# A graph stage of two convolutions and routing: its first norm measured one stage earlier, four row buffers, a pipeline three steps deep

## What is computed

```python
x = x + _L0_gnn_ref(_layernorm(x), adj, ...)      # attention over adj, and an MLP
x = x + _L0_ffn_ref(_layernorm(x), ...)           # slice attention
x = x + _L1_gnn_ref(_layernorm(x), ..., adj, adj)  # two graph convolutions
x = x + _L1_ffn_ref(_layernorm(x), ...)           # shared expert and top 2 of 8 experts

def conv(x, w_rel, w_root, b):                    # in _L1_gnn_ref
    out = jnp.einsum('bnd,de->bne', x, w_root) + b
    for r in range(R):
        agg = jnp.einsum('bij,bid->bjd', masks[r], x) / deg[r]
        out = out + jnp.einsum('bjd,de->bje', agg, w_rel[r])
    return out
h = jax.nn.elu(conv(encoded_spans, w_rel1, w_root1, b1))
h = jax.nn.elu(conv(h, w_rel2, w_root2, b2))
```

## Time and profile before

| what | us |
|---|---|
| median of three executions | 3094.94 |
| span of the profiled execution | 3076.7 |
| attention and MLP stages | 0 to 785 |
| slice stage | 785 to 1654 |
| graph stage, with the shared part | 1654 to 2339 |
| schedule, experts, combine | 2339 to 3077 |

### The profile page before, as it was taken

The page is one execution under the profiler, slowest core; times in us unless marked ns, Lnnn a source line. Parts: engine busy times, 40 slices in busy tenths (PEclk is TensorE's granted clock), DMA queues, the critical chain, the costliest instruction groups (busy, mean ns, idle before and its releaser), DMA issues. The chain is left out here.

```text
span 3076.7 us, 86393 instructions
## 1 busy us (share of the span) xinstructions
PE 2732.4 (89%) x28365; PEld 2234.3 (73%) x28366; DVE 1965.2 (64%) x6886; ACT 1490.2 (48%) x2994; POOL 1438.8 (47%) x2156
## 2 busy tenths in 40 slices
PE   8999999999799999999996777777567999999798
PEld 4666665799577777777775777667456888888687
DVE  5666665677787888878884677777633444444332
ACT  3444454555465666656563444444333444444343
POOL 5555554333233333333332477677730555555543
PEclk9999999999999999999998777777678999999899
DMA  1111111000000000000000111112301222222254
GB/s 48 34 34 34 34 31 28 1 0 0 1 0 0 0 0 0 0 0 0 0 0 22 31 44 50 42 50 85 88 24 53 75 70 75 74 70 76 70 156 133
DMA packets 158078, 117.85 MB, mean 38 GB/s; under 512 B 20150, under 2 KB 145593, under 8 KB 158010
## 3 DMA queue, kind: packets, MB, share of 16 engines
q1 hardware_dynamic: 140602, 81.02, 9.6%
q0 software_dynamic: 17408, 35.95, 3.4%
HBM read 68.36 MB, written 48.56 MB: 38 GB/s over the span
## 5 line engine op out<-in xcount | busy, mean ns | idle before, releaser
L781 POOL TENSOR_TENSOR s_sw<-s_expo,s_rsum 128x512 f32<-128x512 f32 x128 | 133.5, 1043 | 491.8 <-DVE s_rsum L1026 491.8
L1873 ACT ACTIVATE e_hidden<-e_ps,e_b1g 128x512 f32<-128x512 f32 x288 | 191.6, 686 | 286.4 <-PE e_ps L61 192.6
L1851 POOL DMA_INDIRECT token_y<-e_y,e_rows x288 | 283.1, 983 | 78.0 <-issue 69.0
L1239 POOL DMA_INDIRECT sorted_z<-r_z,r_rows x256 | 258.5, 1010 | 75.4 <-issue 75.4
L1907 PE MATMUL e_ps<-expert_w,e_hidden 128*128 x2304 | 284.9, 276 | 7.8 <-issue 7.6
L1907 PEld LDWEIGHTS e_ps<-expert_w,e_hidden 128*128 128x128 f32 x2304 | 276.2, 192 | 15.6 <-issue 9.3
L427 DVE TENSOR_REDUCE a_V<-a_ps_s 128x8 f32<-128x1024 f32 x128 | 156.9, 1226 | 175.2 <-PE a_ps_s L366 175.2
L291 ACT ACTIVATE a_probT<-a_ps_st 128x1024 f32<-128x1024 f32 x128 | 131.1, 1024 | 202.5 <-PE a_ps_st L374 202.5
L366 PEld LDWEIGHTS a_ps_s<-a_nT 16*128 16x128 f32 x2048 | 135.9, 187 | 91.4 <-issue 55.5
L1948 DVE TENSOR_TENSOR e_biased<-e_ps,expert_b 128x512 f32<-128x512 f32 x72 | 49.8, 692 | 234.8 <-remote 120.2
L366 PE MATMUL a_ps_s<-a_nT 16*128 16x128 f32 x2048 | 185.1, 299 | 11.3
(11 more groups left out here) (399 smaller groups left out, 8114.1 us busy)
## 6 DMA issues: line engine op xcount, KB each, us to landing
e_z<-sorted_z SPq DMA_DIRECT2D x72, 260.0 KB
c_y<-token_y SPq DMA_DIRECT2D x22, 512.0 KB, 4.1
X<-in_x_dram SPq DMA_DIRECT2D x32, 256.0 KB, 2.8
a_adj<-in_adj_dram SPq DMA_DIRECT2D x32, 256.0 KB, 2.8
g_adj<-in_adj_dram SPq DMA_DIRECT2D x32, 256.0 KB
out_dram<-X SPq DMA_DIRECT2D x32, 256.0 KB
c_y_s<-token_y SPq DMA_DIRECT2D x10, 512.0 KB
token_y<-e_y,e_rows POOLq DMA_INDIRECT x288
```

The costliest lines, as they stand in the source:

```text
L781: nc.gpsimd.tensor_tensor(sw[p][:, :, :], expo[p][:, :, :], rsum[p][:, 1, :].unsqueeze(2).to_broadcast([T, HEADS, C]), ALU.mult).then_inc( ...
L1239: nc.gpsimd.indirect_dma_start(sh.sorted_z, bass.IndirectOffsetOnAxis(ap=rows[p][:, e * GB + piece:e * GB + piece + 1], axis=0), zr[p][:, ...
L1851: nc.gpsimd.indirect_dma_start(sh.token_y, bass.IndirectOffsetOnAxis(ap=rows[p][:, b:b + 1], axis=0), y[p][:, b, :], None).then_inc(y_scat ...
L1873: nc.scalar.activation(hidden[p][:, c, :], ps_1[c % 2][:, :], ACT.Gelu, bias=b1g[p][:, c:c + 1]).then_inc(s["hidden_done"], 1)
```

## The change

In the slice stage, `bn_stats` and `bn_aggr` of graph t-7 (whose X is complete) are added to DVE's list between z and the maximum of the scores, with a copy of the mean; POOL makes its rstd (two one-column instructions at the end of its step). Mean and rstd are kept in `sh.mean_in` and `sh.rstd_in`. `LAG` goes from 6 to 7.

In the graph stage the first norm is no longer measured: `z` is normalised for group t+1 with those values. Edges and degrees are made one step ahead (group t+1). In one step all of the first convolution and the start of the second (to y2 and root2) are done for group t; gather2, ELU, the add to X, the second norm, `zr` and the router for group t-1; places, rows and the first pair of scatters for group t-2; the other three pairs for group t-3. `LAG` goes from 6 to 3. X is added by one DVE instruction of 128x512. ELU becomes max(Exp(-Relu(-s)) - 1, s), one Relu fewer, in place. `zr`, `rows` and `rdeg` have four buffers, and steps are laid out in rounds of four (`run_rounds`). The running count `taken` becomes `carry`, one add a group; what was added within a group is now summed by PE with small matmuls. rstd of POOL has 4 columns instead of 8. `shared(0)` comes with step 32.

```diff
+def run_rounds(eng, step, count, lag, peel):
+    for t in range(peel):
+        step(t, t // 4, t % 4, t)
+    with eng.Fori(0, (count - peel) // 4 - 1) as i:
+        for k in range(4):
+            step(i * 4 + (peel + k), i + peel // 4, k, None)
+    for t in range(count - 4, count + lag):
+        step(t, t // 4, t % 4, t)
...
# slice stage, POOL, at the end of a step
+                if live(known, 7, n_graphs):
+                    pool.wait_ge(s["after_done"], t - 6)
...
+                    nc.gpsimd.tensor_tensor(after_eps[1 - p][:, :], after[1 - p][:, 1:2],
+                                            sh.eps[:, 0:1], ALU.add).then_inc(s["after_eps_added"], 1)
+                    pool.wait_ge(s["after_eps_added"], t - 6)
+                    nc.gpsimd.tensor_tensor(sh.rstd_in[:, bass.ds(t - 7, 1)], after_eps[1 - p][:, :],
+                                            sh.half_power[:, 0:1], ALU.pow).then_inc(s["after_rstd_done"], 1)
...
# slice stage, DVE, between z and the maximum of the scores
+                if live(known, 7, n_graphs):
+                    dve.wait_ge(s["x_done"], t - 6)
...
+                    nc.vector.tensor_copy(spare[:, :], sh.eps[:, 0:1])
+                    last = nc.vector.bn_stats(stats[:, 1, :], X[:, bass.ds(t - 7, 1), :].squeeze(1))
                 if live(known, 0, n_graphs):
-                    nc.vector.bn_stats(stats[:, :], X[:, bass.ds(t, 1), :].squeeze(1)).then_inc(s["stats_done"], 1)
+                    last = nc.vector.bn_stats(stats[:, 0, :], X[:, bass.ds(t, 1), :].squeeze(1))
...
+                if live(known, 7, n_graphs):
+                    nc.vector.bn_aggr(after[q][:, :], stats[:, 1, :]).then_inc(s["after_done"], 1)
+                    dve.wait_ge(s["after_done"], t - 6)
+                    nc.vector.tensor_copy(sh.mean_in[:, bass.ds(t - 7, 1)], after[q][:, 0:1])
...
# graph stage
-        LAG, PEEL = 6, 8
+        LAG, PEEL = 3, 8
...
# POOL
+            def step(t, r, k, known):
+                if live(known, 3, groups):
+                    scatter((k + 1) % 4, 1)
+                    scatter((k + 1) % 4, 2)
+                if live(known, 1, groups):
+                    pool.wait_ge(s["meanvar_done"], t)
...
+                    nc.gpsimd.tensor_tensor(var_eps[:, :], meanvar[1 - k % 2][:, :, 1],
+                                            sh.eps[:, 0:GB], ALU.add).then_inc(s["eps_added"], 1)
+                    pool.wait_ge(s["eps_added"], t)
+                    nc.gpsimd.tensor_tensor(sh.rstd[:, bass.ds((t - 1) * GB, GB)], var_eps[:, :],
+                                            sh.half_power[:, 0:GB], ALU.pow).then_inc(s["rstd_done"], 1)
+                if live(known, 3, groups):
+                    scatter((k + 1) % 4, 3)
+                if live(known, 2, groups):
...
+                    pool.wait_ge(s["rows_done"], t - 1)
+                    pool.wait_ge(s["gates_set"], t - 1)
+                    pool.wait_ge(s["twin_done"], t - 1)
+                    nc.gpsimd.tensor_tensor(spare[:, k % 2:k % 2 + 1], ones[:, :], ones[:, :], ALU.add)\
                       .then_inc(s["spare_done"], 1)
...
+                    scatter((k + 2) % 4, 0)
...
# PE, places of group t-2
+                    nc.tensor.matmul(ps_r[:, 1, :, :], before[:, :], either[:, :, :], start=True, stop=False)
+                    for b in range(GB - 1):
+                        nc.tensor.matmul(ps_r[:, 1, b + 1:GB, :], sh.ones_bf[:, :],
+                                         either[:, b:b + 1, :].to_broadcast([T, GB - 1 - b, EXPERTS]), start=False,
+                                         stop=(b == GB - 2))
+                    for b in range(GB):
+                        last = nc.tensor.matmul(ps_r[:, 2, 0, :], sh.ones_bf[:, :], either[:, b, :], start=(b == 0),
+                                                stop=(b == GB - 1))
...
# DVE
+                if live(known, 1, groups):
+                    dve.wait_ge(s["exp2_done"], t)
+                    nc.vector.scalar_tensor_tensor(out=neg2[:, :, :], in0=neg2[:, :, :], scalar=-1.0,
+                                                   in1=sum2[:, :, :], op0=ALU.add, op1=ALU.max)\
+                      .then_inc(s["elu2_done"], 1)
+                if live(known, 1, groups):
+                    dve.wait_ge(s["elu2_done"], t)
+                    at = X[:, bass.ds((t - 1) * GB, GB), :]
+                    nc.vector.tensor_tensor(at, at, neg2[:, :, :], ALU.add).then_inc(s["x_done"], 1)
...
+                if live(known, 1, groups):
+                    dve.wait_ge(s["rstd_done"], t)
+                    if since(known, 5):
+                        dve.wait_ge(scattered[(k + 3) % 4], (r - 1 + (k + 3) // 4) * 2 * GB * 16)
+                    nc.vector.tensor_copy(sh.mean[:, bass.ds((t - 1) * GB, GB)], meanvar[q][:, :, 0])
+                    normalized(zr[(k + 3) % 4][:, :, 0, :], t - 1, meanvar[q], sh.rstd, s["zr_done"])
```

More of the change, by code:

```diff
@@ L1250, in _, with scatter @@
-            run_steps(pool, step, groups, LAG, PEEL)
-            for p in range(2):
-                pool.wait_ge(scattered[p], groups // 2 * 2 * GB * 16)
+            def scatter(own, piece):
+                for e in range(2):
+                    nc.gpsimd.indirect_dma_start(
+                        sh.sorted_z,
+                        bass.IndirectOffsetOnAxis(ap=rows[own][:, e * GB + piece:e * GB + piece + 1], axis=0),
+                        zr[own][:, piece, e, :], None).then_inc(scattered[own], 16)
@@ L1255, in _ @@
+            run_rounds(pool, step, groups, LAG, PEEL)
+            for i in range(4):
+                pool.wait_ge(scattered[i], groups // 4 * 2 * GB * 16)
         @block.tensor
@@ L1393, in step @@
-                if live(known, 0, groups):
-                    pe.wait_ge(s["edge_done"], t + 1)
-                    if since(known, 1):
-                        pe.wait_ge(s["degree_done"], t)
-                    for b in range(GB):
-                        last = nc.tensor.matmul(ps_deg[:, b:b + 1], edge[p][:, b, :], ones[:, :], start=True, stop=True)
-                    last.then_inc(s["degree_summed"], 1)
-                if known is not None and known >= groups + 2:
-                    shared(known - groups - 2)
@@ L1402, in _ @@
-            run_steps(pe, step, groups, LAG, PEEL)
-            for u in range(LAG - 2, EARLY + 3):
+                if known is not None and known >= groups:
+                    shared(known - groups)
+            run_rounds(pe, step, groups, LAG, PEEL)
+            for u in range(LAG, EARLY + 3):
                 shared(u)
@@ L1493, in step @@
-                if known is not None and known >= groups + 2:
-                    shared(known - groups - 2)
-            run_steps(act, step, groups, LAG, PEEL)
-            for u in range(LAG - 2, EARLY + 3):
+                        act.wait_ge(s["logits_done"], t - 1)
+                    nc.scalar.activation(zrT[:, :], ps_z[:, :], ACT.Copy).then_inc(s["zrT_done"], 1)
+                if live(known, 0, groups):
+                    act.wait_ge(s["h_turned"], t + 1)
+                    if since(known, 1):
+                        act.wait_ge(s["root2_done"], t)
+                    nc.scalar.activation(hT[:, :], ps_h[:, :], ACT.Copy).then_inc(s["hT_done"], 1)
@@ new lines, in step @@
+                if live(known, 0, groups):
+                    act.wait_ge(s["root2_done"], t + 1)
+                    if since(known, 1):
+                        act.wait_ge(s["elu2_done"], t)
+                    nc.scalar.activation(sum2[:, :, :], ps_r2[:, :, :], ACT.Copy).then_inc(s["root2_copied"], 1)
+                if known is not None and known >= groups:
+                    shared(known - groups)
+            run_rounds(act, step, groups, LAG, PEEL)
+            for u in range(LAG, EARLY + 3):
```

541 lines of the change are left out of this document (243 added, 298 removed).

## The result

The changed kernel takes 3143.63 us (3132.28 to 3144.19) against 3093.67 (3091.46 to 3095.27) for the kernel before on the same chip: a ratio of 1.0159, 95% interval 1.0136 to 1.0183. It is 50 us slower where 39 us less were forecast, and lies outside the range that was given.

What follows compares the result with a forecast made beforehand. The prediction took a ring of POOL (scatters, adds to X, rstd) and DVE (measuring) to bound the graph loop, not PE. From 3094.94 us, +10 + 2 - 6 - 2 - 43 = -39 gave 3056 us, range 2998 to 3093.

Steps and rivals of the forecast that it cites:

- Slice stage: Slice stage: 0.53 us of new DVE work a step, mostly hidden in waits, 0.08 a step left over: +10 us.
- rival D: Slice stage: new DVE work not hidden, delaying L1013 in full, 68 us replacing 10: 3114 us; chance 0.10.
- The ring of POOL and DVE: Graph loop before: POOL's scatters, adds to X and rstd plus DVE's measuring set the 16.5 us step; the change breaks it.
- rival C: Graph loop: chain 0.7 us longer, as by DVE held up by POOL, step 17.1 us, +22: 3078 us; chance 0.20.
- The full-clock step of 13.5 us: Graph loop: the dependent chain of one step, at TensorE's higher clock, becomes the new bound at 13.5 us.
- a low stretch of 3.4 or 6.8 us: Graph loop: TensorE's clock falls every step, costing 1.7 or 3.4 us; mean step 16.4 us, loop -6 us.
- the "long" case: Graph loop: a step with the 6.8 us stretch at low clock, costing 3.4 us: 16.9 us, expected in most steps.
- Rival B: Graph loop: clock falls rarely or briefly, step 14.5 us, another -59: 2997 us; chance 0.20.
- The step that failed: Graph loop: POOL's scatters, rstd, small instructions and hand-overs summed to 13.0 us a step, its adds to X gone.
- The drain: After the graph loop: last group's first transpose of z to first shared matmul falls from 79.6 to 37 us: -43 us.
- rival E: Drain: not shortened, as the shared part waits for a last use or a scatter, +43: 3099 us; chance 0.05.
- The prologue and the longer drain of the slice stage: Prologue loses the first norm, -2 us; slice-stage drain gains one stats, aggregate and POOL pair, +2 us.

Runs made afterwards that it cites:

- e17: Changed kernel with mean copied by POOL, unread matmuls in five PE gaps and pauses of two products between scatters: 2987.03 us, 0.972 of the kernel before.
- e16: Changed kernel with one-product pauses between scatters, mean copied by POOL and unread matmuls in five PE gaps: 3013.14 us, 0.979 of the kernel before.
- e13: The same kernel as e16, in another session: changed kernel with pauses, mean by POOL and five PE gaps filled; 3041.20 us, 0.984 of the kernel before.
- e8: Changed kernel with pauses between scatters, mean copied by POOL and unread matmuls in two PE gaps: 3002.09 us, 0.986 of the kernel before.
- e2: Kernel before, with POOL issuing its eight scatters of a graph step in one run ahead of its four adds: 3113.87 us, 1.012 of the kernel before.
- e14: Changed kernel with one-product pauses between scatters and the slice-stage mean copied by POOL: 3060.92 us, 0.990 of the kernel before.
- e15: The changed kernel itself, run again on the chip of e14: 3141.14 us, 1.015 of the kernel before.
- e4: Changed kernel with only the slice-stage copy of the mean moved from DVE to POOL: 3101.47 us, 1.009 of the kernel before.
- e5: Changed kernel with a product nobody reads on POOL as a pause ahead of two scatter pairs: 3031.88 us, 0.996 of the kernel before.
- e7: The changed kernel itself, run again on the chip of e5: 3033.05 us, 0.997 of the kernel before.
- e10: The same kernel as e2 (kernel before, eight scatters in one run) on another chip: 3036.67 us, 0.999 of the kernel before.
- e11: The changed kernel itself, run again on the chip of e10: 3032.90 us, 0.997 of the kernel before.
- e1: Changed kernel with scatters in runs of four at most, one pair held back until DVE has added X: 3105.06 us, 1.010 of the kernel before.
- e3: Kernel before with the changed slice stage, which measures the first norm though nothing uses it: 3098.32 us, 1.007 of the kernel before.
- e18: The same kernel as e8 (pauses, mean by POOL, two PE gaps filled) on another chip: 3035.31 us, 0.986 of the kernel before.

## Why the prediction was wrong, point by point

**The base.** The 18.2 us that were taken as lying outside the span don't: 1.7 do. The profiled execution was one of some 3078.4 us, not of 3094.94. No term hangs on it, as the forecast starts from the median.

**Slice stage: +24.5, not +10. The term was mis-sized, the mechanism right.** The new work was sized rightly, 0.53 us: from z to the maximum took 0.82 us plus a wait before, and takes 1.34. Its cover was not. The free time is the wait itself, 0.22 and 0.45 us; I had added 0.11 of start-up overlap. So 0.31 us is uncovered in one step and 0.08 in the next: 0.19 on average, which is what the step grew by (0.16 on D), against the 0.08 taken. The bound of 68 for no cover at all (rival D) wasn't reached.

**The loop's order of work: right as far as it went.** The ring of POOL and DVE is gone and POOL has time to spare. X's add takes 691 to 694 ns at L1617 in all 32 groups on A, so the mechanism of rival C (DVE held up by POOL) isn't there in this operation. (The 17.1 us that rival C calls the step of before is that of the middle of its loop; the mean is 16.5.) The Trainium skill, "SBUF — State Buffer", in "The DVE blocks DMA trap", has DVE and GpSimd share a pair of ports that one of them can lock; by these numbers that cost the add nothing here. The full-clock step of 13.5 us was near: e17's steps with the clock at 1.00 take 13.9 to 14.7 us once routing is in them, with the added matmuls in PE's list, and e16's first three steps, which have little routing, 13.5 to 13.9.

**The clock: mechanism right, weight wrong.** Where nothing was held, the clock was no worse than before (0.77 against 0.74 on D). The rule on gaps in the Trainium skill, "TensorE: Matmul & The Clock Gate", "HAM oscillation", would have it so: PE's longest idle time in the loop, once routing is in it, is 2.3 us on D against 5.7 before. But the clock fell in every step all the same, and the step wasn't shorter than before. The forecast had a low stretch of 3.4 or 6.8 us, giving a step of 15.2 or 16.9, and took 16.4. On C and D nearly every step has a low stretch of 6.8 us or, in eight or nine of 32, of 10.2, which no case had; the step is 17.02 and 17.05 us, the "long" case within 0.2 us. Some 31 x 0.6 = 19 us were lost by counting on short ones. Rival B (step 14.5, clock near 1) had a real effect in view, but it takes filler to get it: e13, e16 and e17 have the clock, e8 shows that a little filler isn't enough.

**What none of the cases had: completions of PE held up behind runs of scatters.** The step that failed is the one that costs POOL: "POOL then needs 10.5 + 0.2 + 1.03 + 0.2 and about 1.1 of hand-overs, 13.0 us a step". It counted the scatters' time and not their order; POOL did get its spare time, but PE's messages came late. Before, an add to X followed each pair. Taking the adds away leaves six in a row, and on a chip of the kind of A, B, E and F this holds PE's messages for up to 2.9 us, and ACT's start on zT in 26 of 32 steps. The other 60 us of the loop are this: 19.0 us a step against 17.05 on D, and 19.14 against 17.03 within chip E. The held time is only a part of it, as the clock falls once more: a step with 2.4 us held often takes 20.5 us and has two low stretches of 6.8 us, and the loop has 48 low stretches on A against 32 on D, for a clock of 0.72 and not 0.77. The experiments show the cause from three sides: bringing it into the kernel before (e2), curing it (e14 against e15 on one chip, with e4 for the mean alone), and finding it absent, with the cure idle, where the chip doesn't do it (e5, e7, e10, e11). On such a chip the change is worth -8 to -11 us: the forecast less what the slice stage and the clock took.

**The drain: right.** 43 us were forecast, 40.0 and 41.3 measured; rival E is out. The prologue and the longer drain of the slice stage, -2 and +2, came to -1.4 and -2.0.

**Open.** Why B, E and F (and A) hold completions and C and D don't, and whether that belongs to the chip or to the session; what in the chip holds them; and what the step would be at full clock with none late, as no kernel with five gaps filled ran on C or D. A rival stands untested: every execution on record has its span and granted clock, so all may have run while the profiler was recording, and the missing records show that the recording itself suffers beside scatters on just these chips. No run tells whether the messages would be late without it.

## What to carry to other kernels

An operation on one engine may also be what spaces out that engine's DMA issues: when one is removed from between them, cost the run of issues that is left, not only its time, and look for "remote" waits in the page, also in stages that the change doesn't touch. New work beside a wait is covered for as long as the wait lasts and not longer, so take each step's own wait. A gain or loss of 2% may belong to one chip: compare on more than one before a mechanism is settled.

## What the runs showed of the hardware

- On A, B, E and F the semaphore of a finished PE group is raised up to 2.9 us late in the changed kernel, and up to 6.2 us in e2, while GpSimd issues indirect DMAs one behind the other (0.96 us each, 0.30 between). In the changed kernel on A half of the late ones come 1.1 to 1.3 us behind the end of a scatter's issue, in e16 0.5 to 1.1. The matmuls themselves go on. In the graph loop none of DVE's and ACT's messages that have a record was late.
- How many are held depends on the run and on the speed of PE: none with runs of two to four at a granted clock of 0.74 to 0.78 (before, e1, e3), 45 to 50 of 383 with runs of six at 0.71 to 0.73, 72 of 379 with eight at 0.76, 10 with pauses at 0.77, 25 with the same pauses at 0.82 (e18), 102 and 103 at 0.95, 20 with pauses twice as long at 0.94.
- On the same chips 20 to 33% of the semaphore records due within 1.5 us of a scatter's start are missing in the graph loop, and at most 4% of the others there; on C and D one at most is missing in a trace.
- It goes with the chip as well: the kernel before took 3093.67, 3074.03, 3092.82 and 3076.65 us on A, B, E and F, which hold them, 3043.94 and 3040.96 on C and D, which don't.
- Matmuls that nobody reads raised the clock in the loop from 0.76 or 0.77 to 0.94 or 0.95 when they stood in five gaps of a step, and only to 0.80 or 0.82 in two.
